# Local attention: masked scores kept with queries on partitions, softmax weights scaled and then turned, in place of two score products and a product with ones

## The reference

```
h = shift_token(x); q, k, v = split(h @ wqkv, 3)          # 8 heads of 64
q = l2norm(q) * q_scale;  k = l2norm(k) * k_scale;  q, k = rotary_xpos(q, k)
# windows of 64 queries; keys are the window itself and the one before it
sim = einsum('bhwid,bhwjd->bhwij', 8 * q, k)
mask = (i < j) | (i > j + 64) | (j == -1)
attn = softmax(where(mask, -max, sim));  out = einsum(attn, v)
x = x + out @ wo                                          # then a gated MLP
```

## Time and profile before

| | us |
|---|---|
| median of 3 runs | 1604.53 (1602.49 to 1604.54) |
| the profiled execution's own time | 1612.81 |
| its span, first to last instruction | 1611.0 |
| PE / DVE / ACT / POOL busy in the span | 1359.4 / 1066.6 / 876.1 / 717.6 |
| mean granted TensorE clock | 0.918 of 2.4 GHz |
| attention of local layer 0 | 754.1 to 1095.1 |
| attention of local layer 1 | 1178.3 to 1518.0 |

### The profile page before, as it was taken

How to read it: one execution, slowest core, us unless ns; L and a number is a source line. 1 busy time by engine, 2 the same in 40 slices (tenths; PEclk the granted TensorE clock), 3 DMA queues, 4 the chain that set the end, 5 groups by cost and what they waited for, 6 DMA issues and landing times. The chain is left out here.

```text
span 1611.0 us, 25780 instructions
## 1 busy us (share of the span) xinstructions
PE 1359.4 (84%) x8020; PEld 880.5 (55%) x8020; DVE 1066.6 (66%) x2480; ACT 876.1 (54%) x1779; POOL 717.6 (45%) x635
## 2 busy tenths in 40 slices
PE   6799999745269996597899999997968999999887
PEld 3233333333157775243577777773646777777465
DVE  1399999564068776465777777743667777776264
ACT  5533332242044553175587777765647777777474
POOL 0153544156712556311554444455554444445263
PEclk9899999856579999598699999999979999999999
DMA  4600000031110221401000000000000000000001
GB/s 120 230 1 1 1 0 1 16 103 43 50 64 12 70 75 32 158 1 48 1 2 2 1 0 1 0 2 0 1 21 1 2 2 0 1 0 1 1 1 52
DMA packets 35449, 44.90 MB, mean 28 GB/s; under 512 B 5668, under 2 KB 25281, under 8 KB 35344
## 3 DMA queue, kind: packets, MB, share of 16 engines
q1 hardware_dynamic: 30736, 35.22, 6.8%
q0 software_dynamic: 4608, 8.47, 1.7%
HBM read 23.60 MB, written 21.12 MB: 28 GB/s over the span
## 5 line engine op out<-in xcount | busy, mean ns | idle before, releaser
L1657 POOL TENSOR_TENSOR R<-R,rn 128x512 f32<-128x512 f32 x128 | 130.8, 1043 | 242.5 <-ACT rn L1851 242.2
L1948 DVE TENSOR_TENSOR R<-bank,tab 128x1024 f32<-128x1024 f32 x128 | 151.5, 1220 | 125.7 <-ACT sq L1843 125.3
L1650 POOL TENSOR_TENSOR R<-R 128x512 f32<-128x512 f32 x128 | 162.0, 1287 | 92.2 <-DVE R L1948 92.2
L1194 POOL DMA_INDIRECT expert_rows<-Yt,xin x80 | 83.1, 1039 | 111.2 <-DVE Yt L1167 84.9
L1883 ACT ACTIVATE PT<-bank 128x320 f32<-128x320 f32 x256 | 97.2, 431 | 48.5 <-PE bank L1762 47.7
L616 DVE TENSOR_TENSOR_SCAN S<-beta,U 128x512 f32<-128x512 f32 x64 | 100.0, 1583 | 0.0
L1969 DVE CUSTOM_DVE_ANT_0 masked<-bank,mask_q 128x192 bf16<-128x192 f32 x256 | 90.2, 352 | 0.0
L1967 DVE CUSTOM_DVE_ANT_0 masked<-bank,mask_q 128x128 bf16<-128x128 f32 x256 | 73.2, 286 | 22.5 <-PE bank L1731 12.2
L1843 ACT ACTIVATE sq<-bank 128x512 f32<-128x512 f32 x128 | 75.3, 592 | 20.4 <-PE bank L1687 16.9
L887 POOL DMA_INDIRECT expert_slots<-tok_rows,dst x64 | 64.1, 1001 | 34.1 <-issue 20.3
L1955 DVE TENSOR_REDUCE ss<-sq 128x16 f32<-128x1024 f32 x64 | 77.4, 1209 | 0.0
(11 more groups left out here) (326 smaller groups left out, 3934.9 us busy)
## 6 DMA issues: line engine op xcount, KB each, us to landing
expert_slots<-empty SPq DMA_DIRECT2D x8, 650.0 KB, 6.4
xin<-expert_slots SPq DMA_DIRECT2D x8, 650.0 KB
expert_rows<-empty SPq DMA_DIRECT2D x8, 512.0 KB, 6.7
pair_rows<-expert_rows SPq DMA_DIRECT2D x16, 256.0 KB, 4.2
expert_raw<-w1e_dram SPq DMA_DIRECT2D x9, 256.0 KB, 2.9
expert_raw<-w2e_dram SPq DMA_DIRECT2D x9, 256.0 KB, 3.0
tok<-x_dram SPq DMA_DIRECT2D x8, 256.0 KB, 4.5
out_dram<-tok_out SPq DMA_DIRECT2D x8, 256.0 KB, 2.5
```

The costliest lines, as they stand in the source:

```text
L1194: nc.gpsimd.indirect_dma_start(k.ys[:, :], bass.IndirectOffsetOnAxis(ap=ids, axis=0), Yt[:, s % 3, t, :], None, bounds_check=2 * T - 1, oo ...
L1650: nc.gpsimd.tensor_tensor(halves[:, :, 0, :, z, :], halves[:, :, 0, :, z, :], halves[:, :, 1, :, 1 - z, :], ALU.add).then_inc(summed, 1)
L1657: nc.gpsimd.tensor_tensor(x, x, scale.to_broadcast([P, HEADS, DH]), ALU.mult).then_inc(normed, 1)
L1948: nc.vector.tensor_tensor(R[:, i, qk, :, :].rearrange("p c (h d) -> p c h d", d=DH), x, y.to_broadcast([P, 2, HEADS, DH]), ALU.mult).then_ ...
```

## The change

The scores are made once, in float32, with queries on partitions, in 64 x 64 quarters of the array: for each of the four windows of a sequence and each of two heads, 64 queries by 128 keys (its own tile of keys, in an order that lets one mask constant serve). VectorE's custom reduction now also writes the masked, negated scores, scaled by 1/norm of q (q is no longer scaled by GpSimd; the factor 8 and the sign are in q's table), to a ring `W` of four pairs, and its minimum per row becomes the bias of ScalarE's exponential, which also gives the row's sum. VectorE takes the reciprocal, GpSimd scales the weights, TensorE turns them (4 transposes per pair), ScalarE copies them to `PT`, and TensorE multiplies them with the values, 256 columns per head; the window that needs the second half of one key tile and the first of another uses values that GpSimd has put together in `VM`. VectorE copies the sums to `OT`. The output product is made in two halves of 256 columns, into bank 7, and added in two halves. The lags of the parts are now 6 (scores), 7 (maxima, exponentials), 8 (reciprocals, scaling), 9 (turn and copy), 10 (values) and 11 (sums). The float32r scores, the mask and maxima products, the product with ones, the logarithm of the denominators, the rounded copies, the split and turned maxima, and three of the loads (`sel`, `mT` twice) with three GpSimd memsets are gone.

```diff
@@ prepare_loads, prepare_split, retention @@
-    if l == 0:
-        for t, n in ((k.sel, "rowsel"), (k.mT[0], "eyes"), (k.mT[1], "eyes")):
-            sp.dma_start(t[:], k.dram[n]).then_inc(k.raw_in, 16)
-    pool.wait_ge(k.raw_in, 16 * (4 * l + 7))
+    pool.wait_ge(k.raw_in, 16 * 4 * (l + 1))
@@ staged @@
+                back, p = -((blk - lag) // NPAIR), (blk - lag) % NPAIR
+                alive = (project, attend, finish)[back]
+                return (g - back, (par, 1 - par, par)[back], p) if alive else None
@@ gpsimd @@
+                def scale_weights(c, p):
+                    wait_alone(k, pool, rden_r, NPAIR * c + p + 1)
+                    x = W[:, p % RING, :].rearrange("p (a b) -> p a b", a=4)
+                    scale = rden[:, p % RING, :].rearrange("p (a o) -> p a o", o=1)
+                    nc.gpsimd.tensor_tensor(x, x, scale.to_broadcast([P, 4, P]), ALU.mult).then_inc(scaled, 1)
+                        sc = staged(*now, blk, 8)
+                        if sc:
+                            scale_weights(sc[0], sc[2])
+                        if blk == 0 and attend:
+                            scale_keys(g - 1, 1 - par, NTILE - 1)
+                        elif blk % 2 == 0 and blk and project:
+                            scale_keys(g, par, t - 1)
+...
+                        if blk % 2 and project:
+                            add_halves(g, t)
@@ tensor @@
+                def scores(c, par, p):
...
+                    need(pe, max_r, NU * c + 2 * p)
+                    for blk, tiles in enumerate((slice(0, 2), slice(0, 2), slice(2, 0, -1), slice(2, 4))):
+                        for i in range(2):
+                            rows = slice(DH * i, DH * (i + 1))
+                            o = s * SEQ + blk * WIN
+                            keys = QK[par][rows, NB + b, s * SEQ:(s + 1) * SEQ].rearrange("p (a w) -> p a w", w=WIN)[:, tiles, :]
+                            r = blk % 2 * WIN
+                            m = nc.tensor.matmul(ps[BS[i]][r:r + WIN, blk // 2 * P:(blk // 2 + 1) * P],
+                                                 QK[par][rows, b, o:o + WIN], keys, start=True, stop=True)
+                def turn_weights(c, p):
+                    q = NPAIR * c + p
+                    pe.wait_ge(scaled, q + 1)
+                    need(pe, pt_r, q - 1)
+                    for a in range(4):
+                        m = nc.tensor.transpose(ps[BT[p % 2]][:, a * P:(a + 1) * P], W[:, p % RING, a * P:(a + 1) * P],
+                                                k.const["ident"][:])
@@ scalar @@
+                def weights(c, p):
+                    for i in range(2):
+                        act.wait_ge(max_r, NU * c + 2 * p + i + 1)
+                        for t in range(2):
+                            x, j = W[:, p % RING, (2 * i + t) * P:(2 * i + t + 1) * P], 2 * i + t
+                            m = nc.scalar.activation(x, x, ACT.Exp, scale=-1.0, bias=nm[:, p % RING, j:j + 1],
+                                                     accum_out=den[:, p % RING, j:j + 1])
+                    m.then_inc(exp_r, 1)
@@ vector @@
+                        for t in range(2):
...
+                            m = nc.vector.tensor_tensor_reduce(W[:, p % RING, j * P:(j + 1) * P], ps[BS[i]][:, cols],
+                                                               k.const["mask_q"][:, cols], rn[:, par, 2 * s + t, h:h + 1], FAR,
+                                                               ALU.add, ALU.min, nm[:, p % RING, j:j + 1])
+                def reciprocals(c, p):
+                    dve.wait_ge(exp_r, NPAIR * c + p + 1)
+                    nc.vector.reciprocal(rden[:, p % RING, :], den[:, p % RING, :]).then_inc(rden_r, 1)
```

More of the change, by code:

```diff
@@ new lines, in step @@
+                def step(g, par, project, attend, finish):
+                    now = (g, par, project, attend, finish)
+                    for blk in range(2 * NTILE):
+                        t = blk // 2
+                        sc = staged(*now, blk, 8)
[5 more added lines that the diff above has]
+                            scale_keys(g, par, t - 1)
+                        if blk == 2 and attend:
+                            wait_alone(k, pool, scaled, NPAIR * (g - 1) + 3)
+                            if project:
+                                wait_alone(k, pool, normed, NTILE * g + 1)
+                            mix_values(g - 1, 1 - par, 1)
+                        if blk == 6 and project:
+                            wait_alone(k, pool, normed, NTILE * g + 3)
+                            mix_values(g, par, 0)
+                        if blk % 2 and project:
+                            add_halves(g, t)
@@ L1784, in turn_maxima @@
-                def turn_maxima(c, half):
-                    pe.wait_ge(max_r, NU * c + NPAIR * (half + 1))
-                    wait_alone(k, pe, hl_r, 2 * c + half + 1)
-                    for t in range(2):
-                        m = nc.tensor.transpose(ps[BM][DH:DH + P // 4, :].bitcast(BF16)[:, t * P:(t + 1) * P], hl[half][:, t, :],
-                                                k.const["identb"][:])
-                    m.then_inc(mT_mm, 1)
-                def output(c, par, n):
-                    if n is not None:
-                        pe.wait_ge(rotated, 2 * n + 2)
-                    else:
-                        pe.wait_ge(qk_r, 2 * NTILE * (c + 1))
-                    pe.wait_ge(o_r, NPAIR * (c + 1))
+                    if b == 1:
+                        need(pe, resid, SPC * c + s)
@@ L2277, in constants @@
     i = np.arange(P)[:, None]
-    low = -1e30
-    j = np.arange(KW)[None, :]
-    q0 = (j - WIN >= 0) & (j - WIN <= i) & (j - WIN >= i - WIN)
-    q1 = (WIN + j <= P + i) & (WIN + j >= P + i - WIN)
-    c["mask_q"] = np.where(np.concatenate([q0, q1], 1), 0, low).astype(bf)
-    rows = np.zeros((P, HEADS, 3, P), f)
-    for piece in range(3):
-        q, key = np.arange(WIN)[:, None] + piece * WIN, np.arange(P)[None, :]
-        rows[:WIN, :, piece] = np.where((key <= q) & (q <= key + WIN), 0, low)[:, None]
-    for h in range(HEADS):
-        rows[DH + h, h] = rows[DH + HEADS + h, h] = 1
-    c["rowsel"] = rows.astype(bf)
-    c["eyes"] = np.concatenate([np.tile(eye[:DH, :DH], (1, SEQ // DH)), np.zeros((DH, SEQ), f)]).astype(bf)
+    far = 1e30
+    j = np.arange(P)[None, :]
+    near = (j <= i) & (j >= i - WIN)
+    turned = np.where((i < WIN) & (j >= WIN), j - WIN >= i, near)
+    c["mask_q"] = np.where(np.concatenate([near, turned], 1), 0, far).astype(bf)
     half = D0 // 2
```

350 lines of the change are left out of this document (141 added, 209 removed).

## The result

The changed kernel takes 1582.26 us (median of 4 runs, 1580.52 to 1586.63) against 1603.51: a ratio of 0.9867, interval 0.9849 to 0.9885. It is 21 us faster where 64 were forecast (1540, range 1490 to 1590). The profiled execution took 1581.83 us, span 1580.0.

A forecast was written before the change was run, and what follows sets the result against it. TensorE bound the kernel before; afterwards a loop through all engines would, at 35.2 us per step. Savings of 2 x (23.4 + 0.5) + 2.1 + 12 + 2 = 64 us gave 1540 us, range 1490 to 1590.

The forecast's parts named there:

- its loop: Chain through all engines in full attention steps: 7.05 + 4w, 8.75 us per two blocks, 35.2 per step against 39.1.
- Busy for 31 of 35 us is much nearer to the first.: TensorE's clock in full steps: expected like the steady steps at granted clock 1.00, not the projection-only step at 0.59.
- rival (d): TensorE's waits and transposes drop its clock to 1.2 GHz: 30.7 becomes 61 per step, 1604 + 300 us; chance 0.03.
- The output's 3.1 falls into waits of this loop.: TensorE's output product in a full step: its 3.1 us was claimed to add nothing to the 35.2.
- w: ScalarE's price per 128-column exponential with bias and row sum: 0.42 us taken, 0.29 to 0.62 possible.
- Project-only step: Step that only projects, 33.3 us before: chain taken as unchanged, 0 plus or minus 2 us.
- Tail of layer 0: After layer 0's last projection: GpSimd's weight splitting ends last, 35.3 us instead of 37.4, 2.1 won.
- Tail of layer 1: After layer 1's last projection: 25.4 us instead of 37.46, 12 won; TensorE's own rest about 24.5.
- Loads: Three DMAs ahead of the first gate go: 2 us won, bounds 0 and 2.4.
- (a): TensorE's work binds instead of the chain through all engines, 31.7 us per step: gain 113, 1492 us; chance 0.2.
- (b): Quarter score products don't run four at a time: 1568 us at two, 1645 one by one; chance 0.17.
- (c): ScalarE's exponential row sum makes it slower: 1633 us at w = 0.6, deciding at about 0.54; chance 0.1.

The follow-up runs named there:

- Filling the waits: Three unread 512-column TensorE products added per odd block: on the changed kernel with passes unrolled 1515.69 us (0.9646), with its hardware loop 1554.63 us (0.9696).
- written out: Changed kernel with the three hardware-loop passes of two full attention steps unrolled: 1543.57 us, ratio 0.9813 to the kernel before.
- values first: Changed kernel with ScalarE copying the values ahead of the exponentials in odd blocks: 1496.28 us, ratio 0.9516 to the kernel before.
- made late: Changed kernel with half output products moved behind the weighted values, passes unrolled and three extra TensorE products per odd block: 1503.94 us, ratio 0.9566.
- splitting early: Changed kernel with GpSimd splitting the layer's own experts' weights at the start of the first step with attention: 1545.06 us, ratio 0.9827.
- before written out: Kernel before the change with its three passes of two attention steps unrolled, as a control: 1568.24 us, ratio 0.9975.

## Why the prediction was wrong

Its direction was right and its loop was right; three places at which the loop meets something else were not.

1. **The step that failed: the clock**, "Busy for 31 of 35 us is much nearer to the first." I had it as all or nothing, full clock or the 61 us of rival (d), at 0.03. In fact TensorE, busy 32.4 of 38.1 with one wait of up to 2.1 us in each pair, falls to 1.2 GHz for 3.4 us about once a step, and in the first step with attention for longer. A value in between stood in the earlier trace rows: 0.86 in the first step with attention, which the prediction passed over. Filling the waits gives 1543.57 to 1515.69 = 28 us written out, and 0.9886 to 0.9696, 30 us, with the loop. That is two thirds of the 43 us that were missed. Rival (d) named both waits and transposes. It is the waits: values first has as many transposes, and its twelve full steps have one fall between them. The Trainium skill, "TensorE: Matmul & The Clock Gate", HAM oscillation, describes a matmul kernel that goes back and forth between the levels because it waits inside its loop; there it waits 3 to 5 us for DMAs, here at most 2.1 us for a copy of ScalarE. The trace agrees in kind, and shows it with shorter waits.
2. **"The output's 3.1 falls into waits of this loop."** It doesn't: it stands ahead of the scores, which are in the loop. A pair with a product is 0.7 longer than one without, and 0.3 still when it is made late (9.04 against 8.70); 0.9646 to 0.9566 is 12 us.
3. **The start of a pass** wasn't in the sum, because before it costs next to nothing. There it fell into VectorE's wait for the squares (0.4 at most came through); the change put reciprocal and maxima at the head of VectorE's list, for which the exponentials, the next scores and VectorE's own rotation wait. 7 to 8 us. I had asked what hides each edit, and not what the old slack hid of the things that the change leaves alone.

Together 28, 12 and 8 are 48 to 50; without the three the kernel has a ratio of 0.9566, which is 1534 us on the first chip. Forecast: 1540. That the two lie so close is in part luck: below, the projection-only steps gained 6.6 that were forecast at 0, and the tails and loads 5 to 6 less than forecast.

The terms, point by point.

- Full step without them 35.5 (35.2 forecast), first step with attention 34.9 (35.2).
- TensorE at full clock 31.0 (30.7; scores 0.60 against 0.55, values 0.60 against 0.53). ScalarE 28.8 (30; w 0.385 against 0.42). GpSimd 24.6 (25).
- VectorE 31.8 (29 to 30): a maximum with a factor per row and float32 output takes 0.27 from start to start, not 0.21, which is 32 x 0.06 = 1.9; the rotation starts 1.7 after the projection, not 1.6.
- Project-only step: 3.2 and 3.4 less, outside the 0 plus or minus 2; its pairs go from 6.1, 7.8, 7.8, 9.2 to 6.1, 6.8, 6.1, 8.9, which fits the alternating banks, but no run tested that.
- Tail of layer 0: GpSimd ends last, as forecast, 37.0 instead of 35.3 because its last scaling comes at 20.7 (1062.0 is its end), not 19.2; shown by splitting early.
- Tail of layer 1: 28.1 for 25.4, a gain of 9.4 for 12; there TensorE's last product ends at 1484.0 and VectorE's addition at 1484.5, behind GpSimd's last piece (1483.7), as forecast, but at 27.5 in place of the 24.5 that the prediction gave TensorE's rest without a row.
- Loads: 2 were forecast, about 1 came: from GpSimd's last addition ahead of the stage to its last gate product it is 78.7 us before (662.40 to 741.12) and 77.5 after (652.42 to 729.95). That is one execution of each; on another chip the first projection comes at 714.4 after and at 714.3 in before written out, so the gain isn't shown. The wait for a load is still there, only its name has changed; from the waits of the kernel after, to be set beside the earlier trace rows:

```profile
POOL wqkv_hi L1297 <- DMA vec<-vec_dram: 9.4, 1, 9.4
```

The rivals: (a) fell, since the exponentials' place mattered by 60 us and their length by 0.4 a pair. (b) fell at the first timeline. (c) fell with w = 0.385, well under its 0.54. (d) is the nearest to what happened, but with neither its size nor its all or nothing; that the first step would become slower stood in no rival.

## What to carry to other kernels

When a change takes the bounding engine's load away, that engine gets waits, and then its clock is no longer a constant: look at how long its new waits are, expect falls in between "full" and "half", and price them. In a kernel of fixed instruction lists, write down the loop through the engines and, for each engine, the first thing of its list that another one waits for; an instruction that is early in the list and late in need (four exponentials ahead of a copy) cost 60 us here, half of it through the clock, and more than the whole change gained. And whatever only the old slack hid (a loop's edge, an output product) belongs in the sum, though the change doesn't touch it.

## What the hardware showed that I had not expected

- Useless work can pay: 0.7 us of extra products in each odd block (three, 0.23 apart) made the kernel 28 us faster by holding the granted clock at 1.00 (0.95 and 0.86 without, written out).
- Savings came back doubled where they also removed waits: 1.5 us a step of row sums gave 50 us in all instead of 24.
- The first VectorE instruction of a hardware-loop pass of two steps came after 2.2 us in which the profile shows it waiting for nothing (2.19 and 2.18 at the second and third pass of layer 0, 2.15 and 2.31 in layer 1, where the pair grew by 1.4 alone). What it is made of stays open: instruction fetch and the branch itself weren't told apart.
- The readout of an exponential's row sum is 188 ns long in the trace but adds 0.09 us to the spacing (0.385 against 0.29).
- One chip ran the stages ahead of the local layers of the same kernel in 714 us, another in 745, with undisturbed pairs of blocks in the attention alike: absolute times of different chips shouldn't be mixed, ratios and pairs can be.
